# An eight-layer gated network on one core: x is loaded in two parts, the expert gate is computed inside the last attention, and the tile list is marked in two passes per round

## Reference

```python
def _layernorm(x, axis=-1, eps=1e-05):
    m = jnp.mean(x, axis=axis, keepdims=True)
    v = jnp.var(x, axis=axis, keepdims=True)
    return (x - m) / jnp.sqrt(v + eps)

# A and G (16 heads of 16); G adds bias[h, q, k] and the key mask before its softmax
attn = softmax(q_heads @ k_heads.T * scale)
x = x + tanh(g_xattn[i]) * (attn @ v_heads @ Wp.T + bp)     # q from _layernorm(x), k and v from the context

# H, on _layernorm(x)
logits = jnp.einsum('th,eh->te', x, gate_w)
probs = jax.nn.softmax(logits, axis=-1)
topk_w, topk_idx = jax.lax.top_k(probs, TOP_K)
topk_w = topk_w / jnp.sum(topk_w, axis=-1, keepdims=True)
act = jax.nn.silu(x @ w1[e]) * (x @ w3[e])                  # for the 4 experts e of a token
out = sum of topk_w * (act @ w2[e])
x = x + tanh(g_ffn[3]) * out
```

## Time and profile before

| | |
|---|---|
| timed runs | 1526.54, 1520.07, 1522.46 us; median 1522.46 |
| profiled execution | 1533.8 us, span 1531.7 us |
| busy share of the span | TensorE 78%, weight loads 60%, VectorE 61%, ScalarE 33%, GpSimd 15% |
| mean granted TensorE clock | 0.872 of full speed |
| VectorE in attention | maximum and subtraction 0.80 each (533, 534), reciprocal 0.95 and product 0.29 (543, 544), update 0.41, 0.49 and 0.43 (452, 454, 456), query copy 1.00 for two (508), norm 0.73 for two (469) |
| TensorE | turning of a unit in a full round 1.04 to 1.10 (345); queries of G's first tiles 1067.52 to 1069.51 (321) |
| DMA | 2048 KB of rows of the normalised x to memory, 7.5 us to landing |

### The profile page before, as it was taken

How to read it: one execution, slowest core, us unless ns; L and a number is a source line. 1 busy time by engine, 2 the same in 40 slices (tenths; PEclk the granted TensorE clock), 3 DMA queues, 4 the chain that set the end, 5 groups by cost and what they waited for, 6 DMA issues and landing times.

```text
span 1531.7 us, 22666 instructions
## 1 busy us (share of the span) xinstructions
PE 1194.8 (78%) x8578; PEld 913.7 (60%) x8578; DVE 932.2 (61%) x2339; ACT 502.9 (33%) x1118; POOL 236.5 (15%) x210
## 2 busy tenths in 40 slices
PE   4879899976499988875999879897888852899600
PEld 3657588865247644663565768786666651788400
DVE  5898832357827754985545644356899948455343
ACT  2434433331226662540424311232343320344200
POOL 0350034200000010002010000000000001555376
PEclk9999999985699998996999879899899955899855
DMA  9100055200000003000000530000122010455543
GB/s 350 55 1 2 18 149 145 86 1 0 0 0 2 2 1 111 1 1 21 1 21 1 133 134 1 1 1 0 45 82 75 1 55 14 131 162 160 113 130 116
DMA packets 59952, 89.01 MB, mean 58 GB/s; under 512 B 21267, under 2 KB 50829, under 8 KB 57037
## 3 DMA queue, kind: packets, MB, share of 16 engines
q1 hardware_dynamic: 52365, 67.18, 13.3%
q0 software_dynamic: 7488, 20.46, 5.3%
HBM read 60.73 MB, written 26.89 MB: 57 GB/s over the span
## 4 chain that ended last, share of the span: by engine, by line
PE 59%; DVE 24%; ACT 5%; POOL 5%; issue 4%; DMA 1%; another core or an unknown queue 0%; SPq 0%; DVEq 0%; POOLq 0%; ACTq 0%
PE ps L2350 5%; PE ps L1251 4%; POOL hall L2575 4%; PE ps L683 4%; PE ps L696 4%; PE ps L1756 3%; PE ps L359 2%; PE ps L334 2%; PE ps L2364 2%; PE ps L1770 2%; DVE work L543 2%; PE ps L345 2%; DVE work L533 2%; PE ps L1829 2%; DVE x L454 2%
## 5 line engine op out<-in xcount | busy, mean ns | idle before, releaser
L2564 POOL DMA_INDIRECT hall<-hall_rows,tile_idx x80 | 76.3, 954 | 464.0 <-DVE tile_idx L2490 411.2
L334 PE MATMUL ps<-hall,work 128*128 128x308 f32 x256 | 83.0, 451 | 20.3 <-DVE work L508 17.7
L2350 PE MATMUL ps<-big,work 128*128 x320 | 85.5, 391 | 3.4 <-ACT work L2402 3.4
L1691 ACT ACTIVATE work<-ps,work 128x256 f32<-128x256 f32 x128 | 58.9, 473 | 84.6 <-DVE work L1582 84.6
L359 PE MATMUL ps<-work,hall 78*32 78x128 f32 (+1 forms) x2048 | 69.7, 277 | 13.0 <-DVE work L544 9.0
L434 ACT COPY work<-ps 78x1024 f32<-78x1024 f32 (+1 forms) x64 | 64.4, 1006 | 43.9 <-PE ps L345 42.8
L359 PEld LDWEIGHTS ps<-work,hall 78*32 78x32 f32 (+1 forms) x2048 | 52.7, 110 | 37.9 <-ACT work L434 24.3
L543 DVE RECIPROCAL work<-ps 128x128 f32<-128x128 f32 x64 | 60.8, 950 | 16.1 <-PE ps L359 15.5
L345 PE MATMUL ps<-pack_const,work 128*78 128x128 f32 (+1 forms) x512 | 70.3, 282 | 0.0
L2575 POOL DMA_INDIRECT hall<-expert_rows,back_idx x64 | 62.0, 970 | 38.9 <-DMA expert_rows<-work 19.7
L1251 PE MATMUL ps<-work,pack_F 128*128 128x256 f32 x288 | 66.4, 392 | 0.7 <-ACT work L1311 0.7
(11 more groups left out here) (482 smaller groups left out, 2742.1 us busy)
## 6 DMA issues: line engine op xcount, KB each, us to landing
expert_rows<-work SPq DMA_DIRECT2D x40, 256.0 KB
...
hall_rows<-hall SPq DMA_DIRECT2D x2, 2048.0 KB, 10.2
...
```

Source lines behind the costliest of these rows:

```text
L334: mm = nc.tensor.matmul(o, A["qT"][:, c, b * P:(b + 1) * P], KV["kbd"][:, c, b, k * 4 * SC:(k + 1) * 4 * SC], start=True, stop=True)
L2350: mm = nc.tensor.matmul(ps[:, GU_B[j % 2], 0:2 * INTER], MW["xT"][:, j % 2, c * P:(c + 1) * P], big[:, bass.ds(at + c * 2 * INTER, 2 * INT ...
L2564: gp.indirect_dma_start(out=FETCH_BUF[:, j % HT, :], out_offset=None, in_=hall_rows[:, :], in_offset=bass.IndirectOffsetOnAxis(ap=tile_idx ...
```

## The change

**Start.** x comes as the first two tiles of each batch (`FIRST`), then constants, one context layout and gates, pack A, and then the rest of x (`REST`) and the small loads. Statistics, mean and inverse deviation are computed for the first four tiles, and for the other twelve inside A's first round.

**Keys and values.** They get PSUM banks of their own; `kv_ready` is given for each of the four key spreads and once for the values. Scores wait for their own key spread, the first turning of a unit for the values. In A the values of the context stand behind the first queries in TensorE's order. B's maxima move to A's rounds 2 and 3, the inverse to round 4.

**Gate.** TensorE turns the tiles of x as they are (not normalised) in G's last round and behind it, into `XT_ALL` in the space of pack F, and makes logits of them; mean times the column sums of the gate's weights is subtracted. The experts are chosen by these raw logits, without softmax. The exponential and the normalised tiles follow on ScalarE, behind the choice. Ones, triangle, choice and cumulative sums are bfloat16; the constants of H are made by GpSimd long before.

**Marks.** `HOT_LO` is made by one compare over 512, `HOT_AT` by one over 320, and ScalarE multiplies the latter by the token's number into `HOT_HI`. Each tile's expert is counted on 128 partitions and turned by TensorE into one row.

```diff
-            x_tiles = "b (t p) d -> p (b t) d"
-            sp.dma_start(x[:, :, :], ins["x"].rearrange(x_tiles, p=P)).then_inc(sem("x_in"), 16)
+            load_x(FIRST, "x_in")
             sp.dma_start(packs["const"][:, :], ins["const"]).then_inc(sem("const_in"), 16)
...
+            load("A")
+            load_x(REST, "x_rest")
...
+            if L == "G":
+                values_ctx()
             turn_x(0)
             queries(0)
-            pe.wait_ge(s("kv_ready"), 1 + done(L, "kv_ready"))
+            if L == "A":
+                values_ctx()
             scores(0, 0)
...
+                elif L == "G":
+                    pe.wait_ge(s("sub_ready"), nth(i, NU, 2) + done(L, "sub_ready"))
+                    gate_turn(pe, 0)
+                    gate_turn(pe, 1)
                 if i:
                     project(i - 1, 1)
...
+                elif L == "G":
+                    pe.wait_ge(s("sub_ready"), nth(i, NU, 3) + done(L, "sub_ready"))
+                    gate_turn(pe, 2)
+                    gate_logits(pe, 0)
                 weigh_v(i, 2)
                 project(i, 0)
                 turn_p(i, 3)
+            if L == "G":
+                gate_turn(pe, 3)
+                gate_logits(pe, 1)
             weigh_v(HT - 1, 3)
+            if L == "G":
+                gate_colsum(pe)
+                gate_logits(pe, 2)
+                gate_turn(pe, 4)
             project(HT - 1, 1)
...
+            spread_k(0)
             take_q(0)
+            spread_k(1)
+            if L == "A":
+                dve.wait_ge(sem("xT_ready"), 1)
             normed(1)
             shift(0, 0)
+            spread_k(2)
+            spread_k(3)
+            spread_v()
             for n in range(HT):
                 shift(n, 1)
+                if L == "A" and n == 0:
+                    dve.wait_ge(sem("x_rest"), 32)
+                    first_stats(REST)
...
-                if L == "A" and n == 0:
-                    ffn_max_dve(dve)
...
+                if L == "A" and n in (2, 3):
+                    ffn_max_dve(dve, n - 2)
...
+        def gate_turn(pe, n):
+            pe.wait_ge(sem("x_new"), B * (n + 1) + done("G", "x_new"))
+            if n >= 3:
+                pe.wait_ge(sem("xT_ready"), nth(n - 3, 1, 0) + done("H", "xT_ready"))
...
+        def gate_logits(pe, n):
+            pe.wait_ge(sem("xT_ready"), nth(n, 1, 0) + done("H", "xT_ready"))
...
+            for t in range(NT):
+                nc.scalar.activation(hall[:, t, :], x[:, t, :], ACT.Identity, bias=MW["nm"][:, t:t + 1],
+                                     scale=rstd[:, t, :]).then_inc(sem("xn_ready"), 1)
+            for t in range(NT):
+                act.wait_ge(sem("H_hot"), t + 1)
+                if t >= 2:
+                    act.wait_ge(sem("H_inv_ps"), t - 1)
+                nc.scalar.activation(HOT_HI[:, t % 2], HOT_AT[:, t % 2], ACT.Copy, scale=MW["id"][:, t:t + 1]
+                                     ).then_inc(sem("H_hot_scaled"), 1)
...
-                for k in range(TOP):
-                    loose(ve.tensor_scalar(HOT_LO[:, t % 2, k, :], slots[:, 1:P + 1], lo[:, t, k:k + 1], MW["id"][:, t:t + 1],
-                                           ALU.is_equal, ALU.mult))
...
+                loose(ve.tensor_tensor(HOT_LO[:, t % 2], LO16.rearrange("p (o n) -> p o n", o=1).to_broadcast([P, TOP, P]),
+                                       wide(lo[:, t, :], P), ALU.is_equal))
+                ve.tensor_tensor(HOT_AT[:, t % 2], HI16.rearrange("p (o n) -> p o n", o=1).to_broadcast([P, TOP, NJ]),
+                                 wide(hi[:, t, :], NJ), ALU.is_equal).then_inc(sem("H_hot"), 1)
```

376 lines of the change are left out of this document (218 added, 158 removed), and 8 rows, old and new, of the table TOTALS.

## The result

The changed kernel takes 1488.76 us (median of 1486.18, 1488.41, 1489.11 and 1489.68), the kernel before 1522.25 us beside it: a ratio of 0.9774, 95% interval 0.9749 to 0.9799, some 33.5 us less.

The account below looks back on a forecast made before the run. The bound was taken to change from stage to stage (chain: TensorE 59%, VectorE 24%). Terms -4.9 - 2.7 - 11.2 - 2.8 + 0.5 - 4.9 = -26.0 us took the 1522.46 us median to 1496 us, range 1489 to 1504.

Parts of the forecast that it names:

- Part 3: Gate work inside attention G: G ends 2 us later, 10.8 us left behind the last projection, logits read 11.2 us earlier.
- the rival with a chance of 0.10: Gate's matmuls run at the full clock since they follow attention at once: 10.8 us would halve, 1490.5 us; chance 0.10.
- Part 2: Start of attention G: scores wait for only one key spread and the query copy; -2.7 us (bounds -1 and -4).
- VectorE's idle time: At G's start, VectorE waits of 2.2 and 1.9 us and 0.4 of gaps go, about 1.8 us come.
- Part 1: Start of attention A: pack at 10 us, statistics behind the first update 7.1 us earlier; -4.9 us (bounds -1.5 and -8.5).
- The maxima: Maxima over B's weights, moved to A's rounds 2 and 3: 2.2 us each, half of them showing, +2.2 us.
- I keep its price: In A, VectorE's collision with GpSimd's quantising moves from rounds 1 to 3 into 4 to 6 at unchanged cost.
- Part 4: Choosing experts: no softmax ahead, bfloat16 cumulative additions, -2.8 us; small steps for each tile's expert, +0.5 us.
- Part 5: The marks: 16 rounds go from 1.43 to 1.09 us, less 0.5 at the end; -4.9 us (bounds 0 and -6.5).
- The loss by the formula of the Trainium skill: Objection for the marks: four passes of 128 cost 0.51 us, one of 512 0.59, losing 0.08 a round.
- just make it: ScalarE's 16 normalisations, 0.4 us each, start 7 us before the first marks and finish in time.
- (15.8 - 12.1) / 5: Price of one turn of a tile in the old gate chain behind G, given as 0.72 us.

Follow-up runs that it names:

- gate_late: Changed kernel with all turns, logits and column sums of the gate behind G's last projection, their copies on ScalarE behind G too; 0.9873 of the time before.
- gate_wide: Like gate_late, plus one 512-column matmul with unread result beside the logits of each pair; run once, 1510.9 us.
- after_again: The changed kernel, unedited, profiled again on the same chip as gate_late; span 1496.0 us.
- g_values_early: Changed kernel, but in G alone the values are spread ahead of the first query copy, not behind the fourth key spread; 0.977 of the time before.
- marks_old: Changed kernel with the old marks: four compares of 128, one of 320, no ScalarE pass; 0.9776 of the time before, first marks to list 23.68 us.

## Why the prediction was too small

**Part 3 failed, with the largest term.** The step was "Left behind the last projection are five pairs of logits and three turns, 5 x 1.73 + 3 x 0.72 = 10.8 us". Five pairs and three turns were left, but at the full clock. From the last statistics to the read 5.4 us remained where my steps left 10.0 (23.24 less 13.2), 4.6 us that I had not counted; that is the rival with a chance of 0.10, whose price I had put at 5.5. I held the 0.50 of the earlier trace rows for a property of this work. It hangs on what stands before and beside it: alone for 20 us it had 0.50 (gate_late), with wide matmuls among it 1.00 (gate_wide), and begun inside attention it kept 1.00 for most of what was left (the changed kernel). The other half of the part, that G would end 2 us later by the inserted work, failed in the same direction: on one chip the last round took 11.36 us with the gate work in it (after_again) and 11.45 without (gate_late), counted from the fourteenth statistics of G to the sixteenth. Pairs at 0.96 fitted into the waits. Before, this stretch took 11.44 to 13.49.

**Part 2 failed by its mechanism.** Scores started earlier, as worked out, but "VectorE's idle time" was not given back: it moved behind the values, whose place in VectorE's order I had priced at nothing, and the clock fell in that wait. On one and the same chip 0.6 to 0.9 us were gained at the first update, instead of 2.7; g_values_early, which moves the values, brought another 4.65. Together with the tail G gave -1.2 where I had -0.7.

**Part 1 was of the right mechanism, its terms mis-sized, and it was luck that they nearly cancelled.** The pack came at 13.1 us, outside my bounds of 9 to 12, and at 11.2 to 12.9 in later profiles; the first queries took 3.78 us in ten of the thirteen profiles, not 2.0. So VectorE had the first scores at 24.20 us in the first profile and at 22.7 in the mean, not at 21.3. From there to the first update it took 22.9 us, for my 24. The first update was to be 7.1 us earlier; it was 5.2 in the first profile, 8.0 and 8.4 in the two pairs on one chip (54.02 to 45.98, 53.39 to 44.95), and 7.5 in the mean; the profile that I worked from was the earliest of five there. The maxima show with 3.4 us (2.2 said). What I had not counted is the quantising's place: "I keep its price" was right in eight of fourteen profiles and 4 us too much in five. Where its price was kept, A gained 5.3 us (188.7 to 183.4), near my 4.9; the rest of the mean's 7.0 is the quantising.

**Part 4** gave -2.9 for -2.3; four additions took 1.27 us for 1.3, where float32 took 1.80. With the twice rate of the Trainium skill (VectorE: DVE Perf Modes, the perf-mode tier table) the trace agrees.

**Part 5 was half as large**, -2.6 for -4.9. The idea was right: marks_old gives 2.7 back, and one pass of 512 takes 0.61 us to the next start against 1.11 for four of 128. The loss by the formula of the Trainium skill (VectorE: DVE Perf Modes, the errata section) did not come. But "just make it" was wrong: 16 normalisations take 0.50 each, not 0.4, and wait for the small steps behind the choice, so the marks stalled 1.6 us, and a round took 1.15 with ScalarE's pass at 0.56, not 0.47.

**Outside the sum**: C's 3.0 and B's 0.7 us, and no list-to-end at all. In all -7.0 - 0.7 - 3.0 - 1.2 - 18.0 - 2.9 - 2.6 = -35.4, beside 33.2 to 34.7 by the medians. Of the 9.4 us more than my 26.0 the gate has 4.8 (18.0 for 13.2) and B with C 3.7; the marks had 2.3 less.

Two slips of the prediction changed nothing: (15.8 - 12.1) / 5 is 0.74, not 0.72, and VectorE's terms in Part 1 add to 23.6, which I called 24.
